# Second attention of a four-part transformer kernel: the row maxima move from a matmul of their own into free rows of the stacked operands, and three pieces of work change engines

## The reference

```
c_k = x @ w_dk + b_dk ;  c_v = x @ w_dv + b_dv
k = c_k @ w_uk + b_uk ;  v = c_v @ w_uv + b_uv
q, k, v = split_heads(x), split_heads(k), split_heads(v)      # 16 heads of 8
q, k = apply_rope(q, cos, sin), apply_rope(k, cos, sin)
attn = softmax(einsum('bhid,bhjd->bhij', q, k) / sqrt(8))
out  = einsum('bhij,bhjd->bhid', attn, v) -> (B, T, 128)
return out @ w_o + b_o
```

## Time and profile before

| | |
|---|---|
| median of three runs | 1536.97 us |
| profiled execution, from first to last instruction | 1538.6 us |
| mean granted clock of TensorE | 0.965 of full speed |
| second attention, set-up to first batch | about 867 to 918 us |
| its 16 batches | about 918 to 1321 us |
| TensorE, weight loads, VectorE, ScalarE, GpSimd busy | 1378.3, 1115.1, 1022.5, 914.9, 642.5 us |

### The profile page before, as it was taken

How to read it: one execution, slowest core, us unless ns; L and a number is a source line. 1 busy time by engine, 2 the same in 40 slices (tenths; PEclk the granted TensorE clock), 3 DMA queues, 4 the chain that set the end, 5 groups by cost and what they waited for, 6 DMA issues and landing times. The chain is left out here.

```text
span 1538.6 us, 34900 instructions
## 1 busy us (share of the span) xinstructions
PE 1378.3 (90%) x10621; PEld 1115.1 (72%) x10622; DVE 1022.5 (66%) x3323; ACT 914.9 (59%) x2485; POOL 642.5 (42%) x975
## 2 busy tenths in 40 slices
PE   6999999999999999499999579999999999868876
PEld 5777777777777777378888457777777777656665
DVE  4777777777777777456666588888888886442223
ACT  4656666666666666255555336666676765756653
POOL 1344444444444444423333432345444433335553
PEclk9999999999999999889999779999999999989998
DMA  6111111111111110011111431122115000046635
GB/s 232 59 34 58 39 59 39 60 38 62 36 61 37 65 33 7 15 43 48 48 47 47 157 103 38 47 80 75 41 55 186 9 13 14 12 127 194 183 106 175
DMA packets 64483, 106.95 MB, mean 70 GB/s; under 512 B 11664, under 2 KB 49936, under 8 KB 61920
## 3 DMA queue, kind: packets, MB, share of 16 engines
q1 hardware_dynamic: 54112, 86.50, 18.4%
q0 software_dynamic: 8864, 18.43, 3.5%
q10 hardware_dynamic: 1440, 1.19, 0.3%
HBM read 85.57 MB, written 61.60 MB: 96 GB/s over the span
## 5 line engine op out<-in xcount | busy, mean ns | idle before, releaser
L380 POOL TENSOR_TENSOR a_prob<-a_prob,a_rl 128x128 f32<-128x128 f32 (+1 forms) x256 | 124.2, 506 | 239.4 <-DVE a_rl L477 238.9
L261 ACT ACTIVATE a_prob<-psum,a_nmx 128x128 f32<-128x128 f32 (+1 forms) x512 | 210.4, 423 | 7.8 <-DVE a_nmx L472 7.8
L2146 DVE TENSOR_REDUCE a_mx<-psum 128x2 f32<-128x512 f32 x256 | 170.8, 688 | 37.2 <-PE psum L1470 34.2
L292 ACT ACTIVATE a_probt<-psum 128x768 f32<-128x768 f32 x128 | 103.7, 810 | 130.9 <-PE psum L734 130.9
L1830 ACT ACTIVATE a_prob<-psum 128x1024 f32<-128x1024 f32 x128 | 129.2, 1025 | 12.9 <-PE psum L1502 12.3
L471 DVE TENSOR_REDUCE a_nmx<-psum 128x2 f32<-128x256 f32 x128 | 54.3, 425 | 119.8 <-PE psum L666 119.8
L866 POOL DMA_INDIRECT yt<-m_yrow,m_dest x71 | 68.0, 957 | 146.0 <-DVE m_yrow L986 144.6
L305 ACT ACTIVATE a_ot<-psum,a_bias 128x256 f32<-128x256 f32 x128 | 61.2, 478 | 95.3 <-PE psum L758 90.3
L1470 PE MATMUL psum<-a_k_stk,q_stk 128*128 128x256 f32 x512 | 109.1, 310 | 8.2 <-DVE a_mx L2146 5.1
L734 PE MATMUL psum<-ident,a_prob 128*128 128x128 f32 x768 | 106.7, 275 | 9.8 <-DVE a_prob L481 7.8
L261 ACT ACTIVATION_READ_ACCUMULATOR a_prob<-psum,a_nmx 128x1 f32 x512 | 107.8, 210 | 0.0
(11 more groups left out here) (354 smaller groups left out, 4097.1 us busy)
## 6 DMA issues: line engine op xcount, KB each, us to landing
xs<-in_fill SPq DMA_DIRECT2D x144, 264.0 KB
m_w<-in_wr SPq DMA_DIRECT2D x39, 321.0 KB
a_stage<-in_w SPq DMA_DIRECT2D x16, 384.0 KB, 4.2
m_xrow<-xs SPq DMA_DIRECT2D x39, 132.0 KB
m_xrow<-xs SPq DMA_DIRECT2D x71, 66.0 KB, 1.8
a_yin<-yt SPq DMA_DIRECT2D x16, 256.0 KB, 2.8
f_yin<-yt SPq DMA_DIRECT2D x7, 512.0 KB, 8.6
yt<-m_yrow,m_dest POOLq DMA_INDIRECT x149, 2.2
```

Of the source, the lines that this page charges most:

```text
L261: last = nc.scalar.activation(prob[:, slot, h, at], S[:, 2 * slot + h, at], ACT.Exp, bias=nmx[:, slot, q, h:h + 1], accum_out=lsum[:, slot ...
L292: nc.scalar.activation(probt[:, hp % 2], PT[:, :, 0:SW], ACT.Copy).then_inc(pt_done, 1)
L380: last = nc.gpsimd.tensor_tensor(prob[:, slot, 0, at], prob[:, slot, 0, at], rl[:, slot, 0, q:q + 1].to_broadcast(prob[:, slot, 0, at].sha ...
L2146: nc.vector.reduce_max(mx[:, :, h:h + 1], bank.rearrange("p (q k) -> p q k", q=QB), AX.X).then_inc(mx_done, 1)
```

## The change

The low x low part is left out: a head now takes 24 partitions (BAND), four heads 96 (KR), and partitions 96 to 127 of the operands are free. They hold the maxima. On the q side, which is now copied once per group (q_stk, 4 groups x 256), they hold the 32 rows of turned maxima; on the k side, which is now the masked one (k_stk, 16 heads x 256), they hold ones where the row belongs to the head (markers, written once per buffer by ScalarE from pick). One matmul of 128 rows thus gives score minus maximum, and the matmul with pick is gone. mh becomes 128 columns wide, so that the turned maxima land on partitions 96 to 127; VectorE copies them into group 0 of q_stk, and GpSimd copies them to the other three (spread_maxima). The first scores use rows 0 to 95. The low halves of q and k are subtracted by GpSimd from the fourth batch on (low_halves). Group 1 is masked by ScalarE in the loop, like the others.

```diff
+BAND = 24
+KR = 4 * BAND
             def stack(k, bank):
-                    out = bank[:, j * T:(j + 1) * T]
+                    out = bank[0:KR, j * T:(j + 1) * T]
             def first_scores(h, p, bank):
-                    last = nc.tensor.matmul(bank[:, q * T:(q + 1) * T], q_stk[:, p, h, q * P:(q + 1) * P],
-                                            k_stk[:, p, h // HG, :], start=True, stop=True)
+                    last = nc.tensor.matmul(bank[:, q * T:(q + 1) * T], q_stk[0:KR, p, h // HG, q * P:(q + 1) * P],
+                                            k_stk[0:KR, p, h, :], start=True, stop=True)
             def maxima(n):
-                    last = nc.tensor.transpose(R1[0:2 * H1, q * P:(q + 1) * P], mh[:, q, :].bitcast(F32), g.ident[:])
+                    last = nc.tensor.transpose(R1[:, q * P:(q + 1) * P], mh[:, q, :].bitcast(F32), g.ident[:])
             def scores(t, p):
-                    nc.tensor.matmul(out.rearrange("p (k q) -> p k q", k=QB), pick[:, h:h + 1].to_broadcast([P, P]),
-                                     mt[:, p].unsqueeze(1).to_broadcast([P, QB, T]), start=True, stop=False)
                     for k in range(QB):
-                        last = nc.tensor.matmul(out[:, k * T:(k + 1) * T], k_stk[:, p, h // HG, k * P:(k + 1) * P], q_stk[:, p, h, :],
-                                                start=False, stop=k == QB - 1)
+                        last = nc.tensor.matmul(out[:, k * T:(k + 1) * T], k_stk[:, p, h, k * P:(k + 1) * P], q_stk[:, p, h // HG, :],
+                                                start=True, stop=True)
...
                     scores(1, p)
                     pe.wait_ge(exp_done, n * NPR + 1)
+                    pe.wait_ge(mt_spread, n + 1)
                     scores(2, p)
...
                     outputs(1, p, n)
                     if turned:
-                        pe.wait_ge(stack_dve, n + 3)
+                        pe.wait_ge(stacked[1], n + 3)
                     first(11)
...
                 for j in range(HG):
-                    nc.scalar.activation(q_stk[:, p, k * HG + j, :], bank[:, 0:T], ACT.Identity, scale=in_head[:, j:j + 1])
-                nc.scalar.activation(k_stk[:, p, k, :], bank[:, T:2 * T], ACT.Copy).then_inc(stack_act, 1)
+                    nc.scalar.activation(k_stk[0:KR, p, k * HG + j, :], bank[0:KR, T:2 * T], ACT.Identity, scale=in_head[0:KR, j:j + 1])
+                nc.scalar.activation(q_stk[0:KR, p, k, :], bank[0:KR, 0:T], ACT.Copy).then_inc(stacked[k], 1)
+            def markers(p):
+                nc.scalar.activation(k_stk[KR:P, p], pick[KR:P, :].unsqueeze(2).to_broadcast([P - KR, H1, T]), ACT.Copy)
...
+            act.wait_ge(pick_done, 1)
+            markers(0)
             act.wait_ge(init, 1)
             incoming(columns_of(0), 1)
...
             stacks(3, 0, R1, 1)
+            markers(1)
...
                     exps(5, n)
+                    if turned:
+                        stacks(1, p, R1, n + 3)
                     outputs(1, n)
...
+            def low_halves(n):
+                for j, total, high, signal in ((0, rq, q_high, q_split), (1, rk, k_high, k_split)):
+                    pool.wait_ge(high, n)
+                    nc.gpsimd.tensor_tensor(qk_l[:, j, :], total[:], qk_h[:, j, :].bitcast(F32), ALU.subtract).then_inc(signal, 1)
+            def spread_maxima(p, n):
+                pool.wait_ge(mt_done, n)
+                nc.gpsimd.tensor_tensor(q_stk[KR:P, p, 1:NGR, :], q_stk[KR:P, p, 0, :].bitcast(F32).unsqueeze(1).to_broadcast([P - KR, NGR - 1, T]),
+                                        one[KR:P].unsqueeze(2).to_broadcast([P - KR, NGR - 1, T]), ALU.mult).then_inc(mt_spread, 1)
+                pool.wait_ge(mt_spread, n)
...
                         incoming_power(n + 4)
+                    if within(n + 2):
+                        low_halves(n + 1)
                     if routed:
                         pool.wait_ge(scattered, n * SCATTERS - 2 * SCATTERS)
                     power(n + 1)
...
                         name_rows(1 - half, n)
+                    if within(n + 1):
+                        if within(n + 3):
+                            pool.wait_ge(kcos_done, n + 4)
+                        if routed or n > 0:
+                            pool.wait_ge(kept, n)
+                            pool.wait_ge(named, n)
+                        spread_maxima(1 - half, n + 2)
                     if routed:
                         scatter_rows(half, n - 1, i * (E1 * 16) + 16)
...
                 chain.done(nc.vector.tensor_tensor(total[:], sine[:], cosine[:], ALU.add))
-                chain.done(nc.vector.tensor_copy(qk_h[:, j, :], total[:]))
+                high = nc.vector.tensor_copy(qk_h[:, j, :], total[:])
+                if not ahead:
+                    high.then_inc(signal[3], 1)
+                    return
...
-                nc.vector.tensor_copy(mt[0:2 * H1, p, :], R1[0:2 * H1, 0:T]).then_inc(mt_done, 1)
+                nc.vector.tensor_copy(q_stk[KR:P, p, 0, :], R1[KR:P, 0:T]).then_inc(mt_done, 1)
...
                     maximum(9)
-                    if turned:
-                        stacks(1, p, n + 3)
                     if fresh:
                         incoming_low(columns_of(n + 3), n + 4)
```

More of the change, by code:

```diff
@@ L1288, in attention1 @@
     prob = sb("prob", [P, 2, HG, QB * T])
-    sel = sb("sel", [P, 4, NGR, P], F32R)
-    pick = sb("pick", [P, H1], F32R)
+    sel = sb("sel", [P, 4, NGR, KR], F32R)
+    pick = sb("pick", [P, H1])
     warm = sb("warm", [P, HG])
@@ L1344, in attention1 @@
                for a, b in ((0, W), (W * GT, 2)))
-    hid_h, hid_l = (flat(q_stk[:, 1])[:, a * W * GT:(a + 1) * W * GT].rearrange("p (d n) -> p d n", n=GT) for a in range(2))
+    hid_h, hid_l = (flat(k_stk[:, 1])[:, a * W * GT:(a + 1) * W * GT].rearrange("p (d n) -> p d n", n=GT) for a in range(2))
     TB = NB1 + 1
@@ L1362, in attention1 @@
         "xsin_done", "ksin_done", "xcos_done", "kcos_done", "q_split", "k_split"))
-    stack_ps, stack_act, stack_dve, s1_ps, mx_done, nmx_done, mt_ps, mt_done = (sem(n) for n in (
-        "stack_ps", "stack_act", "stack_dve", "s1_ps", "mx_done", "nmx_done", "mt_ps", "mt_done"))
+    stack_ps, s1_ps, mx_done, nmx_done, mt_ps, mt_done = (sem(n) for n in (
+        "stack_ps", "s1_ps", "mx_done", "nmx_done", "mt_ps", "mt_done"))
+    stacked = [sem(f"stacked{k}") for k in range(NGR)]
     st_ps, exp_done, pv_ps, osb_done = (sem(n) for n in ("st_ps", "exp_done", "pv_ps", "osb_done"))
@@ L1619, in _ @@
             maxima(1)
-            pe.wait_ge(stack_act, 5)
-            pe.wait_ge(stack_dve, 2)
+            for k in range(NGR - 1):
+                pe.wait_ge(stacked[k], 2)
             def batches(i, routed):
@@ L2059, in _ @@
             rotate_k(3)
+            pool.wait_ge(kcos_done, 3)
+            spread_maxima(0, 1)
             def batches(i, routed):
@@ L2242, in tail_store @@
                                         ).then_inc(nt_done, 1)
-            nc.vector.tensor_tensor(pick[:], g.ident[:, 0:H1], g.ident[:, H1:2 * H1], ALU.add)
+            nc.vector.tensor_tensor(pick[:], g.ident[:, KR:KR + H1], g.ident[:, KR + H1:P], ALU.add).then_inc(pick_done, 1)
             dve.wait_ge(th_done, 1)
@@ L2251, in _ @@
             nc.vector.memset(osb[:], 1.0)
-            nc.vector.memset(mt[:].bitcast(F32), 0.0).then_inc(osb_done, 1)
+            nc.vector.memset(mh[:].bitcast(F32), 0.0).then_inc(osb_done, 1)
             incoming_variances(1)
@@ L2576, in layout @@
     a["cos"], a["sin"] = np.cos(angle), np.sin(angle)
-    sel = np.zeros((P, 4, H1 // 4, P), np.float32)
+    sel = np.zeros((P, 4, H1 // 4, KR), np.float32)
     for f in range(P):
         h, e = f // DH1, f % DH1
-        for c in range(4):
+        for c in range(3):
             for j, high in ((0, c in (0, 2)), (1, c in (0, 1))):
-                sel[f, 2 * j + (0 if high else 1), h // 4, 32 * (h % 4) + 8 * c + e] = 1
+                sel[f, 2 * j + (0 if high else 1), h // 4, BAND * (h % 4) + DH1 * c + e] = 1
     a["sel"] = sel.reshape(P, -1)
@@ L2609, in layout @@
     a["rc"] = rconst
-    a["in_head"] = (r[:, None] // 32 == np.arange(4)[None, :]).astype(np.float32)
+    a["in_head"] = (r[:, None] // BAND == np.arange(4)[None, :]).astype(np.float32)
     a["r0w"] = np.ascontiguousarray(np.transpose(inputs["L0_ffn_router_w"]))
```

71 lines of the change are left out of this document (35 added, 36 removed).

## The result

The changed kernel took 1551.41 us (median of 4 runs, 1548.11 to 1552.01); beside it the kernel before took 1537.39 (4 runs, 1536.62 to 1540.13). The ratio is 1.0088, with a 95% interval of 1.0073 to 1.0103. The forecast was 1532 us with a range of 1508 to 1547. The profiled executions have spans of 1549.7 and 1538.6 us, 11.1 us apart.

What follows compares the result with a forecast made beforehand. TensorE looked busiest, but the chain through ScalarE's stacks(1) and head 11 was taken to close the batch at 25.8 us against 26.0. Eleven batches give 1 us, the last two 4: 5 us off, 1532 us, range 1508 to 1547.

Steps and rivals of the forecast that it cites:

- Rival 3: GpSimd's queue is late and TensorE's stack(0) waits for k_split: slower, 1539 to 1547 us; chance 0.22.
- the main case: Looped batch closes through ScalarE's stacks(1) and head 11, 25.8 us against 26.0; 1532 us, own range 1525 to 1539; chance 0.48.
- The wait before head 11: In a looped batch TensorE idles 1 to 2 us before head 11, until ScalarE's last stacks(1) instruction.
- 22.3 + 3.5 = 25.8 us: Batch length: stacks(3) ends at 22.3 after ot, then 3.5 to the next ot; between 25.4 and 26.3.
- stack(3) and its latency are about 0.6: Late in the batch, stacks(2) ends at 19.8, so stacks(3) starts 0.6 us later, at 20.4.
- Half of the loss is absorbed: Of the 1.1 us lost at head 11, half vanishes at stacks(3), which used to wait for the turned maxima.
- So GpSimd arrives just in time: I cost it at nothing.: GpSimd's spread and subtractions end 2.6 to 3.2 us behind ot, stack(0) started at 3.11: cost nothing, cover 0 to 0.5.
- The ends of the attention: First two batches give 0; the last two, without stacks(1), give 2 us each, 4 in all (0 to 7.5).
- rival 5: TensorE's clock falls because the engine waits more: 1560 us or more; chance 0.03.
- The markers: Before the loop, ScalarE's two writes of at most 4.1 us each fall into idle stretches and cost nothing.
- rival 4: Without pick's columns, weight loads of a head's other two matmuls are no longer hidden; nothing comes back, 1537 us; chance 0.06.
- TensorE's busy time down by some 100 us: Sign of being right: removing the pick matmuls (16 x 16 x 0.39) cuts TensorE's busy time while the span hardly moves.

Runs made afterwards that it cites:

- the run with both of GpSimd's jobs relieved: Changed kernel with slots ahead of the turned maxima and the low halves back on VectorE, masking still on ScalarE: ratio 1.0069 to the kernel before.
- the masking alone moved: Kernel before with only group 1's masking in the loop moved to ScalarE, between exps(5) and outputs(1): ratio 1.0090, looped step 26.70 us against 25.47.
- the first pair: The changed kernel and the kernel before as first measured and profiled, ahead of the experiments: 1551.41 against 1537.39 us, ratio 1.0088.
- all three jobs on VectorE: Changed kernel with masking, low halves and the spread (as one wide copy) on VectorE: ratio 0.9937 to the kernel before, looped step 24.80 us.
- the early-masking run: Changed kernel with ScalarE's stacks(1) moved from behind exps(5) to between tail_store and the incoming copy: ratio 0.9996 to the kernel before, second chip.

## Why the prediction was wrong

**The direction.** Rival 3, a slower kernel, had 0.22, and its range ended at 1547. It names GpSimd's queue; the main case's own mechanism did most of the damage, and the queue the smaller part. The chances also don't add up as written: by their own terms they are 0.47 for faster and 0.26 for same, not 0.49 and 0.24.

**The wait before head 11: right in place and size.** "TensorE idle before head 11 for 1 to 2 us, released by the last stacks(1) instruction": 1.56, by that instruction. Head 11 was put at ot + 12.4; it is at 12.64, and at 12.50 in the run with both of GpSimd's jobs relieved. klat was put at 13.7 and is at 13.89.

**The step that failed is the sum behind it: "22.3 + 3.5 = 25.8 us".** In the run with both of GpSimd's jobs relieved, the nearest to the case that I walked, stacks(2) ends at ot + 19.67 (put at 19.8), but stacks(3) starts at 21.44, put at 20.4. "stack(3) and its latency are about 0.6" took only TensorE's time; there the turning of the maxima comes between, with a wait of 0.82 for mh, a copy by VectorE, and 0.23 more before first(0). The kernel before has that wait too, against the prediction's reading that "From there to the end TensorE issues without a wait", and its stacks(3) starts 1.27 us behind the end of stacks(2) (1123.06 to 1124.33):

```profile
1121.97 0.39 PE L1492 MATMUL psum<-ident,a_mh 128*32 128x128 f32 x2 [0.66 <-DVE a_mh L2152]
```

From the end of stacks(3), 23.26, to ot are 2.85, put at 3.5. The two errors are +1.0 and -0.6, and the step is 26.1 instead of 25.8, on a chip where the kernel before does 25.5 and not 26.0. "Half of the loss is absorbed" was thus wrong: with the masking alone moved, the whole 1.1 to 1.2 us of loss before head 11 arrives at the end of the step (26.70 - 25.47 = 1.23). The turned maxima don't absorb it, because they are late as well: with the masking alone moved, the transposes of mh start at ot + 19.06 where they start at ot + 17.87 in the kernel before on that chip, 1.19 us later.

**"So GpSimd arrives just in time: I cost it at nothing."** Its spread takes 1.47 us (put at 1.4), the low halves end at ot + 3.33 (1115.65; 0.17 of wait). The size was right. What was missed is that the spread's start is followed by VectorE's short cast, held for 1.41 instead of 0.17, and with it two maxima: "in my sum it costs nothing, as most of VectorE's work reads PSUM". Most isn't all. Taken away by itself it brought nothing, since stack(0) then waits 0.93 us for the low halves. Together they are 0.5 us in an undisturbed step, by the trace alone.

The contention had been read off, and the prediction took it up for instructions with two SBUF inputs only. Such a case stood in its way already: VectorE's last subtraction for mh takes 0.19 us in the 87 batches of the fourteen traces in which no tensor operation of GpSimd is running when it starts, and 0.59 to 0.74 in the other 137, those of the kernel before included. The Trainium skill, GPSIMD Engine Reference, section Key points, names two kinds of VectorE instructions that contend with GpSimd: those with two SBUF inputs, which the subtraction bears out, and those in a 2-port perf mode. The cast has one input, and was held for 1.2 us beside a GpSimd copy of 32x768; whether it is of the second kind no trace shows.

**The ends of the attention.** "4 us" for the last two batches: 0.3 in the first pair, 0.7 on the first chip of the experiments (40.49 and 39.79). "0" for the first two: 1.7 gained in both (50.61 and 48.89 there). Together 2.0 to 2.4 of the 4 forecast.

**"TensorE's clock falls", rival 5 with 0.03.** It happened, not as a lasting loss of 20 us and more but before the first batch, in a piece that lost 3.0 us in both pairs, and in single steps: three of the ten looped ones have a mean of 0.94 in the first pair.

**The markers** were hidden, at 3.61 us each (bound 4.1). **The weight loads** (rival 4) were too: four second scores take 0.64 us at 1114.07, like the four first scores of the earlier trace rows. **"TensorE's busy time down by some 100 us"** was wrong, 30 came: it summed recorded durations that overlap their neighbours', which by spacing are 60.

The span's 11.1 us in the first pair, put together: +2.9 in the piece at half clock before the first batch, -1.7 in the first two batches, +14.3 in the ten of the loop, -1.5 in the last four, and -2.9 in parts that the change doesn't touch, so that they stand for what two executions differ in there.

## What to carry to other kernels

When work moves between engines, ask where in the other engine's order it lands before asking whether that engine has room. ScalarE was busy 17.84 us of 26; 1.84 more in the wrong place cost 1.5 per step, and moving it ahead of the incoming copy and one exps gave about half of that back by the ratio. And where an edit has two side effects, test them singly and together: here each of two removals alone gave at most 0.2 us per step, and both together 0.5 in the undisturbed steps. A short operation deserves the same question: whether one of another engine is running when it starts.

## What the runs showed of the hardware that was not expected

**The clock before the loop.** Between 910 and 915 us of the trace TensorE had a granted clock of 0.50 in the changed kernel and in all nine variants of it on the two chips of the experiments, and of 1.00 and 0.94 in the kernel before and in its variant with ScalarE's masking. In the first pair the two part at 915 to 916, and the first pick matmul is at 919.57, so it isn't the pick that raised it. Up to there TensorE's instructions in this part match in kind and order; they differ in the rows used (96 of 128 in the first scores), the width of the stacks' output and of mh. Which of these matters wasn't tried. First the kernel before, then the changed one, on the first chip of the experiments:

```profile
912.00:926.00 14.00, 13.38 (x99) 11.20 (x98) 12.53 (x40) 9.91 (x19) 3.49 (x5) 1.00 0.00 1
```

```profile
912.00:926.00 14.00, 12.01 (x57) 10.20 (x56) 10.08 (x31) 6.34 (x12) 4.41 (x5) 0.64 0.01 1
```

Not all of the 2.9 to 3.0 us is clock. GpSimd's first spread stands in this piece, and a VectorE addition that starts beside it is held for 1.43 us. Without that spread (all three jobs on VectorE) it takes 0.15. First the changed kernel, then that run:

```profile
916.70 1.43 DVE L2326 TENSOR_TENSOR sb2m<-a_sb 128x1 f32<-128x1 f32 x1
```

```profile
914.40 0.15 DVE L2312 TENSOR_TENSOR sb2m<-a_sb 128x1 f32<-128x1 f32 x1
```

From klat to the first exps that run needs 10.14 us at half clock, all others with the change 10.51 to 10.53, and the kernel before 7.9 to 8.0 at mostly full clock: some 0.4 us are the held addition. That the clock makes the rest is argued from the half clock and not tested.

**The turns of the loop.** In the first pair's profile of the changed kernel four of the steps that end at a turn of the loop (it runs over batches in pairs) last 28.3 to 28.6 us, the three between them 27.1 to 27.2, and the outer three of the ten 26.1 to 26.7. In three of them ot comes late although the transposes before it are long recorded: ScalarE idles 3.9 us where it idles 2.16 else.

```profile
1001.00 0.39 ACT L1841 ACTIVATE a_ot<-psum 128x256 f32<-128x256 f32 x1 [2.16 <-issue]
...
1029.48 0.38 ACT L1841 ACTIVATE a_ot<-psum 128x256 f32<-128x256 f32 x1 [3.88 <-remote]
...
1056.59 0.39 ACT L1841 ACTIVATE a_ot<-psum 128x256 f32<-128x256 f32 x1 [2.16 <-issue]
```

On the first chip of the experiments this is absent; in the early-masking run on the second it is there (3.05 against 2.16). Three steps with 1.7 us each are some 5 of the first pair's 11 us. The cause is open; no run changed the loop's form.
